# Issuing the negated maxima's row transfers from ScalarE's queue instead of SyncE's

## The reference, cut to what matters

```python
q = (layernorm(x) @ Wq + bq)   # k and v from the context, split into 16 heads
scores = q k^T / sqrt(16)
attn = softmax(scores)
x = x + tanh(g_xattn) * ((attn v) @ Wo + bo)
logits = layernorm(x) @ Wr + br
gate = softmax over the two largest logits
x = x + tanh(g_ffn) * sum over the two of gate * (relu(xn @ W1 + b1) @ W2 + b2)
```

## Time and profile before

| | |
|---|---|
| median of 3 runs | 1002.23 us (1001.48 to 1002.8) |
| the profiled execution's own time | 1005.98 us |
| its span | 1004.1 us |
| PE busy | 832.2 us (83%) |
| DVE busy | 616.5 us (61%) |
| ACT busy | 441.6 us (44%) |
| POOL busy | 377.5 us (38%) |
| granted TensorE clock, mean | 0.92 of full speed |

### The profile page before, as it was taken

The page is one execution under the profiler, slowest core; times in us unless marked ns, Lnnn a source line. Parts: engine busy times, 40 slices in busy tenths (PEclk is TensorE's granted clock), DMA queues, the critical chain, the costliest instruction groups (busy, mean ns, idle before and its releaser), DMA issues.

```text
span 1004.1 us, 21736 instructions
## 1 busy us (share of the span) xinstructions
PE 832.2 (83%) x6483; PEld 542.1 (54%) x6484; DVE 616.5 (61%) x1107; ACT 441.6 (44%) x777; POOL 377.5 (38%) x365
## 2 busy tenths in 40 slices
PE   4788889888888888985047999999999999999920
PEld 3344444444444444433026777777777777777710
DVE  3567666666677677662994556555555655655557
ACT  3456665666666766432503333333333333333300
POOL 2113323333233333102513355555555655555210
PEclk9799998999999999976557999999999999999975
DMA  4324443444444344212451111111111111111159
GB/s 133 101 76 144 130 147 123 144 147 144 139 139 133 119 129 129 61 56 100 134 185 44 42 49 52 47 47 52 47 47 48 51 42 52 47 47 49 36 197 326
DMA packets 104171, 98.81 MB, mean 98 GB/s; under 512 B 9478, under 2 KB 96972, under 8 KB 104012
## 3 DMA queue, kind: packets, MB, share of 16 engines
q1 hardware_dynamic: 92140, 73.75, 23.5%
q0 software_dynamic: 7488, 20.46, 6.7%
q10 hardware_dynamic: 4512, 4.20, 1.2%
HBM read 67.03 MB, written 31.20 MB: 98 GB/s over the span
## 4 chain that ended last, share of the span: by engine, by line
PE 63%; DVE 17%; issue 7%; ACT 4%; DMA 4%; SPq 3%; POOL 1%; DVEq 0%; ACTq 0%; POOLq 0%
PE banks L1359 19%; PE banks L1345 7%; PE banks L1346 7%; PE banks L1347 7%; PE banks L1104 6%; DVE negmax L851 5%; PE banks L1223 3%; PE banks L1203 3%; ACT probs L706 3%; PE banks L1087 3%; PE banks L1161 2%; DVE stats L790 2%; DVE hot_col L986 2%; PE banks L1332 2%; PE banks L1240 1%
## 5 line engine op out<-in xcount | busy, mean ns | idle before, releaser
L1359 PE MATMUL banks<-wall,hh 128*128 x624 | 222.7, 379 | 0.5 <-DVE yb L1038 0.5
L752 ACT ACTIVATE hid<-banks,b_col 128x256 f32<-128x256 f32 x312 | 130.8, 470 | 209.8 <-PE banks L1347 114.2
L851 DVE TENSOR_REDUCE negmax<-banks 128x4 f32<-128x1024 f32 x128 | 155.6, 1218 | 49.5 <-PE banks L1161 48.0
L1345 PE MATMUL banks<-xh,wall 128*128 128x256 f16 x624 | 171.2, 274 | 0.0
L1346 PE MATMUL banks<-xl,wall 128*128 128x256 f16 x624 | 171.1, 274 | 0.0
L1347 PE MATMUL banks<-xh,wall 128*128 128x256 f16 x624 | 171.1, 274 | 0.0
L592 POOL DMA_INDIRECT y_rows<-yb,dest_idx x78 | 106.7, 1368 | 162.7 <-DVE yb L1038 125.5
L1359 PE MATMUL banks<-wall,hl 128*128 x624 | 157.3, 273 | 0.0
L706 ACT ACTIVATE probs<-banks 128x1024 f32<-128x1024 f32 x128 | 125.8, 1023 | 38.7 <-PE banks L1188 38.4
L1036 DVE SCALAR_TENSOR_TENSOR yb<-banks,b_b 128x256 f32<-128x256 f32 x78 | 33.1, 425 | 133.0 <-PE banks L1359 133.0
L1030 DVE TENSOR_TENSOR hl<-hid,hh 128x1024 f16<-128x1024 f32 x78 | 95.6, 1225 | 2.7
(11 more groups left out here) (159 smaller groups left out, 1242.9 us busy)
## 6 DMA issues: line engine op xcount, KB each, us to landing
wst<-in_L_ffn_W SPq DMA_DIRECT2D x32, 512.0 KB, 5.6
ks<-k_parts SPq DMA_DIRECT2D x96, 64.0 KB, 2.4
qs<-q_parts SPq DMA_DIRECT2D x96, 64.0 KB, 2.4
xin<-in_x SPq DMA_DIRECT2D x16, 256.0 KB, 3.2
cin<-in_ctx SPq DMA_DIRECT2D x16, 256.0 KB, 3.8
k_parts<-kparts SPq DMA_DIRECT2D x16, 256.0 KB, 2.3
q_parts<-qparts SPq DMA_DIRECT2D x16, 256.0 KB, 2.3
xres<-in_x SPq DMA_DIRECT2D x16, 256.0 KB, 2.8
```

Of the source, the lines that this page charges most:

```text
L752: ins = nc.scalar.activation(hid[half][:, c % (HC // 2), :], banks[:, b, c % 2 * TS:(c % 2 + 1) * TS], ACT.Relu, bias=b1_col[:, ds(e * HC ...
L851: nc.vector.tensor_reduce(negmax[:, c, 8 * (g // 2):8 * (g // 2) + 8].rearrange("p (m g p2) -> p m g p2", m=2, g=2)[:, :, g % 2, :], banks ...
L1345: nc.tensor.matmul(dst, hi, xh[par][:, m, :], start=(m == 0), stop=False)
L1359: ins = nc.tensor.matmul(dst, h_[:, c, s * P:(s + 1) * P], w_, start=(c == 0 and k == 0), stop=(c == HC - 1 and k == 1))
```

## The change

SyncE's `max_row` goes away, with both of its calls. ScalarE gets a `max_row` with the same two transfers and the same wait. Its first call stands after `attended_T` and ahead of `high(1)`, its second after the exponential of piece 1 and ahead of `context_T`'s copy. What is transferred, the waits of TensorE for it and VectorE's stream are the same.

```diff
@@ SyncE @@
-            def max_row(n, par, s):
-
-                hold(sp, nm_evac, 2 * n + s + 1)
-                for m in range(2):
-                    a = HALF_ROWS * m + KR
-                    sp.dma_start(qs[par][a:a + 1, 4 * s:4 * s + 4, :], negmax_row[s][4 * m:4 * m + 4, :]).then_inc(row_full[s], 16)
-
...
                 if ahead:
                     store_part(n + 1, 1 - par, "k")
-                max_row(n, par, 0)
                 if ahead:
                     load_part(n + 1, 1 - par, "k")
                 if ahead:
                     store_part(n + 1, 1 - par, "q")
-                max_row(n, par, 1)
                 if ahead:
                     load_part(n + 1, 1 - par, "q")
@@ ScalarE @@
+            def max_row(n, par, s):
+                act.wait_ge(nm_evac, 2 * n + s + 1)
+                for m in range(2):
+                    a = HALF_ROWS * m + KR
+                    act.dma_start(qs[par][a:a + 1, 4 * s:4 * s + 4, :], negmax_row[s][4 * m:4 * m + 4, :]).then_inc(row_full[s], 16)
+
...
                 if post:
                     attended_T(n - 1)
+                max_row(n, par, 0)
                 if weights:
                     high(1)
                 for v in range(8):
...
+                    if v == 1:
+                        max_row(n, par, 1)
                     if ahead == 2 and v == 1:
                         context_T(n + 2)
```

## The result

| | before | after |
|---|---|---|
| median | 1002.8 us | 1006.69 us |
| lowest to highest of 13 runs | 1001.1 to 1006.81 | 1003.67 to 1009.01 |
| profiled execution, its own time | 1005.98 us | 1003.67 us |
| its mean granted clock | 0.92 | 0.926 |

The ratio is 1.0032, with a 95% interval of 1.0017 to 1.0046: slower by 3.2 us (1.7 to 4.6), a third of a per cent (the two medians themselves differ by 3.9). On the 1002.23 from which the forecast went that is 1005.4.

The account below looks back on a forecast made before the run. TensorE held 63% of the chain, ScalarE 4%. Batch 1's 0.53, two times 0.59 for batches 14 and 15, and batch 0's 0.2 gave 1.9 us on the 1002.23 median: 1004.1 us, range 1001.9 to 1006.4.

Parts of the forecast that it names:

- likeliest case: Three batches pay for a pair and batch 0 a little; chance 0.58, its own range 1002.9 to 1005.4 us.
- within 0.2%: Whole kernel: time not distinguishable from no change, up to a line at 1004.2 us; chance 0.52.
- ScalarE's price for a pair: Both row transfers issued by ScalarE: 0.60 us each as on SyncE, 1.20 to 1.25 a pair, bounds 0.90 and 1.34.
- Loop bodies: 0.: Both pairs in 12 loop batches cost 0: delays of 0.33 and 0.6 us are hidden, the latter by TensorE's `xn` wait.
- Batch 1: 0.53: Second pair in batch 1, without the `xn` wait: the exponential of piece 2 delays `attend` 2, costing 0.53 us.
- Batches 14 and 15: 0.59 each: Second pair there: exponential 2 and `attend` 2 move, so `scores` 4 starts at 426.83 instead of 426.24.
- Batch 0, first pair: 0.2: TensorE waits for this transfer; SyncE's six loads may run over ScalarE's pair, costing 0 to 0.47 us, taken as 0.2.
- Rival 1, the queues take turns: In batch 0 each ScalarE issue waits for one SyncE load; first pair 0.94 late, sum 2.6, 1004.9 us; chance 0.08.
- Rival 2, the loop pays: Second pair at `norm_T` in 12 loop bodies costs once a pair takes 2.0 us; 1012, half 1007; chance 0.08.
- Rivals 3 and 4: 3: pair takes 0.9, nothing measurable, 1002.9 us, chance 0.18. 4: freed SyncE brings work sooner, 999.7 us, chance 0.08.

Follow-up runs that it names:

- The repeat: The changed kernel as it is, timed once more in the last group against the kernel before; 1008.3 us, ratio 1.0046.
- loop-only kernel: Against the kernel before, ScalarE issues both pairs only in the loop's batches 2 to 13, SyncE in the written-out ones; 1003.94 us, ratio 1.000.
- loads-after kernel: The changed kernel, with SyncE's loads of k starting only after the first set's rows have landed; 1006.71 us, ratio 1.0025 to the kernel before.
- half-each kernel: Against the change, SyncE issues the first transfer of each pair and ScalarE the second; 1002.82 us, ratio 0.9998 to the kernel before.
- first-pair: Against the kernel before, only the first pair is issued by ScalarE, in all batches, the second stays with SyncE; 1007.0 us, ratio 1.004.
- doubled kernel: The changed kernel, with two more row transfers to spare device memory behind the second pair in batches 1 to 13; 1018.78 us, ratio 1.014.

## Why the prediction was right, and where not

- **Sign and size.** Forecast +1.9 us; measured +3.2 (1.7 to 4.6), or 1005.4 on its base, inside its range and at the upper end of its likeliest case's own. The repeat's 1.0046 would be 1006.8 on that base, just above the range. The sum was too low in every term but the loop's. That the result still lies inside is owed to the width of the range and not to the terms. More chance was on "within 0.2%" (0.52) than on "slower" (0.40); it is slower.
- **ScalarE's price for a pair**, taken from SyncE's: 1.20 and 1.21, right, but for the first one of the program.
- **Loop bodies: 0.** Right, shown by the loop-only kernel's 1.000. The first exponential came 0.32 late (0.33 forecast), the wait for `xn` shrank to 0.70 (about 0.8 forecast), and the body stayed. The detail that the rows land 1.1 after the issue and before VectorE releases `scores` 0 was wrong: they take 1.73, and TensorE waits 0.26 for them. That this made `scores` 0, and the exponential behind it, late by as much as `high(1)` does is a coincidence. In the loads-after kernel, where `scores` 0 doesn't wait for rows, the exponential still starts 3.42 after them (201.63 to 205.05), so `high(1)` does it alone.
- **Batch 1: 0.53** forecast, 0.57 measured.
- **Batches 14 and 15: 0.59 each** forecast, 0.71 and 0.67 measured. The term was sized a little low: I started exponential 2 right at the pair's end (425.13 to 425.2), and ScalarE gets going 0.10 us after it (424.07 to 424.17), and in batch 14 `scores` 4 follows `attend` 2 at 0.65, not 0.58, since the rows release it, 1.82 after their issue. In batch 15 it is 0.58 (451.15 to 451.73), as forecast.
- **Batch 0, first pair: 0.2** (0 to 0.47) forecast, about 1.0 measured. This is the step that failed, by its size. "0 if the two don't touch, 0.47 if the pair has to let one load by" bounded a collision of issues, and the pair is as long without the loads as with them. In its place stand two things, both outside the bounds: the first row transfer of ScalarE's queue takes 1.20 instead of 0.59, whoever is beside it, which makes the pair 0.48 longer than SyncE's, and the rows land 0.67 later beside the six loads. Both were unseen in the trace before, where ScalarE issued no such transfer and the loads came after the pair. I had bounded the price of an issue by the nearest rows, all of them later ones or SyncE's; I had not bounded the landing at all.
- **Rival 1, the queues take turns.** Its number, a sum of 2.6, was nearer than mine, but ScalarE's wait for the other queue, by which it came to that, is refuted: 0.61 and 0.59 side by side at 421.5 in the half-each kernel, and 1.82 without any load beside it. That its sum came nearer is luck. The rule of the Trainium skill that stood behind it (Perfetto Trace Analysis, section DMA Instruction — HWDGE), by which one of two queues would show the wait for a shared descriptor generator, doesn't show in these rows. Two rows could be read by it, 1.52 for ScalarE's first row transfer beside SyncE's 0.69 and 1.30 for SyncE's load in the change's batch 0; no run here tells whether they are.
- **Rival 2, the loop pays.** Not at 1.2 us a pair. Its threshold of 2.0 us was right as nearly as it could be tested: held for 2.06 us (324.58 to 326.64), a body grows by 0.1.
- **Rivals 3 and 4** fell: a pair took 1.20, not 0.9, and TensorE's waits for rows rose from 3.8 to 10.3 us instead of falling.

What stays open: why ScalarE's first row transfer is long; why rows land later beside SyncE's loads, and not always; and whether an edit lowers the clock or only meets it low. The batches of the change account for 2.9 of the 3.2 us, but the repeat of it, the first-pair and above all the doubled kernel lost more than their batches account for.

## What to carry to other kernels

A transfer that is issued from a computing engine's queue costs that engine the whole issue, here 0.59 us each, though the page of the profile books it as idle. Before moving one, look in each differently shaped stage (first, last and steady batches) for the wait that will swallow it: here the same move cost nothing in twelve batches and 0.6 to 1.0 us in each of the other four. And count issues before choosing their queue: one transfer for both halves took 0.52 where two took 1.20, and a half on each queue cost nothing measurable.

## What the runs showed of the hardware

- The first row transfer from ScalarE's queue was issued in 1.15 to 1.21 us, in every profile where it was taken apart, later ones in about 0.6. In the half-each kernel it took 1.52, with SyncE's (0.69) at the same moment. A transfer of the same size from another tile, 22 us earlier, took 0.63 and changed nothing of it. For SyncE the first pair read 1.34 and later ones 1.20.
- Past the first, two queues issue at the same time without slowing each other (0.61 and 0.59). But rows mostly landed later beside the other queue's six loads of 64 KB: in batch 0 a pair 1.76 us after its issue against 1.09 without them, in a loop body 1.73, in batch 14 a pair 1.82 and a single transfer 1.83.
- In these three forms the issue's time did not go by the size: 0.59 for a transfer of 2 KB between tiles, 0.52 for one of 4 KB that covers two target partitions, and some 0.4 for one of 2 KB to device memory.
- Stretches at half the TensorE clock lengthened single loop bodies from 27.0 to about 29.3 us, two in the profile before and one in that after. The executions of one kernel go with it: 997.39 us at a mean clock of 0.934, 1006.92 at 0.920 (both before, in the last group). Where such a stretch lies moved an edit's effect in a batch by 0.4 us (0.67 at `scores` 0, 0.25 at the batch's end).
